# An attention block on one core: layer-norm tokens turned by VectorE, DMA and GpSimd in place of TensorE, and 231 blocks of exponentials on VectorE in place of 204

## The reference, cut to what matters

```python
h = _layernorm(x, axis=-1) * (1 + ca) + sa
q = jnp.einsum('bte,fe->btf', query, Wq)...          # query is h; k and v likewise
scores = jnp.einsum('bhtd,bhsd->bhts', q * scaling, k)
attn_w = jax.nn.softmax(scores, axis=-1)             # 4 x 32 x 2048 x 2048 exponentials
aw = aw[:, :, 0] - lam * aw[:, :, 1]
attn = jnp.einsum('bhts,bhsd->bhtd', aw, v)          # then an RMS norm per head pair, Wo
x = x + ga * attn_ref(h, ...)
h = _layernorm(x, axis=-1) * (1 + cb) + sb
x = x + gb * jnp.einsum('bsi,oi->bso', h, w_ternary * scale)
```

## Time and profile before

| what | us |
|---|---|
| median of 3 runs | 3610.86 (3609.04 to 3613.66) |
| the profiled execution, its own time | 3607.35 |
| its span in the profile | 3605.5 |
| ACT busy in it | 3534.4 (98%) |
| PE busy | 3405.9 (94%) |
| DVE busy | 2588.9 (72%) |
| POOL busy | 338.0 (9%) |

### The profile page before, as it was taken

How to read it: one execution, slowest core, us unless ns; L and a number is a source line. 1 busy time by engine, 2 the same in 40 slices (tenths; PEclk the granted TensorE clock), 3 DMA queues, 4 the chain that set the end, 5 groups by cost and what they waited for, 6 DMA issues and landing times. The chain is left out here.

```text
span 3605.5 us, 76890 instructions
## 1 busy us (share of the span) xinstructions
PE 3405.9 (94%) x32302; PEld 799.1 (22%) x32302; DVE 2588.9 (72%) x3808; ACT 3534.4 (98%) x2808; POOL 338.0 (9%) x229
## 2 busy tenths in 40 slices
PE   8999999999899999999999999999999999989998
PEld 5222112122122222222222222222221222211222
DVE  6687878863578687776367768677547888878886
ACT  5999999999999999999999999999999999999998
POOL 3010101010010100101001010100100000000001
PEclk9999999999999999999999999999999999999999
DMA  6111110111101111101111001111012110010000
GB/s 196 28 32 39 32 31 22 35 39 33 38 21 42 48 35 40 50 23 33 36 47 50 25 31 36 40 49 36 20 31 63 45 37 22 17 30 16 20 22 26
DMA packets 103700, 136.90 MB, mean 38 GB/s; under 512 B 9916, under 2 KB 88716, under 8 KB 103340
## 3 DMA queue, kind: packets, MB, share of 16 engines
q1 hardware_dynamic: 102524, 131.01, 12.9%
q10 hardware_dynamic: 816, 0.79, 0.1%
HBM read 72.50 MB, written 59.19 MB: 37 GB/s over the span
## 5 line engine op out<-in xcount | busy, mean ns | idle before, releaser
L1146 ACT ACTIVATE probs<-ps 128x1536 f32<-128x1536 f32 (+1 forms) x2732 | 3497.4, 1670 | 15.5 <-PE ps L1263 13.9
L1291 PE MATMUL ps<-probs,values 128*32 128x512 f32 x14600 | 2047.9, 606 | 4.9 <-DVE wmod_sb L1644 2.4
L1263 PE MATMUL ps<-queries,keys 25*128 25x512 f16 x7680 | 1003.9, 385 | 160.6 <-ACT probs L1146 142.0
L1263 PEld LDWEIGHTS ps<-queries,keys 25*128 25x128 f16 x7680 | 249.8, 91 | 1947.3 <-ACT probs L1146 1861.5
L1291 PEld LDWEIGHTS ps<-probs,values 128*32 128x32 f32 x14600 | 300.2, 108 | 416.9 <-issue 410.5
L1623 DVE TENSOR_SCALAR d_y<-ps 128x512 f32<-128x512 f32 x240 | 165.6, 690 | 295.4 <-PE ps L1263 284.7
L1708 DVE STREAM_TRANSPOSE seg_t<-ps 128x512 f32<-128x512 f32 x127 | 91.0, 716 | 356.9 <-PE ps L1291 356.4
L1060 POOL TENSOR_TENSOR seg_rs<-seg_ms,neg_half 128x16 f32<-128x16 f32 x64 | 185.7, 2901 | 1506.1 <-DVE seg_ms L1721 1506.1
L1640 DVE SCALAR_TENSOR_TENSOR wmod_sb<-wmod_sb 128x1024 f32<-128x1024 f32 x204 | 249.6, 1224 | 6.3
L1644 DVE SCALAR_TENSOR_TENSOR wmod_sb<-wmod_sb,gates 128x1024 f32<-128x1024 f32 x204 | 249.5, 1223 | 6.0
L1642 DVE SCALAR_TENSOR_TENSOR wmod_sb<-wmod_sb,d_y 128x1024 f32<-128x1024 f32 x204 | 249.3, 1222 | 5.3
(11 more groups left out here) (181 smaller groups left out, 1690.9 us busy)
## 6 DMA issues: line engine op xcount, KB each, us to landing
v_scr<-a_v SPq DMA_DIRECT2D x16, 1024.0 KB, 5.6
values<-v_scr SPq DMA_DIRECT2D x29, 512.0 KB
queries<-q_scr SPq DMA_DIRECT2D x116, 96.0 KB
keys<-k_scr SPq DMA_DIRECT2D x116, 96.0 KB
e_x<-in_x_dram SPq DMA_DIRECT2D x18, 512.0 KB, 5.2
attn_scr<-seg_o SPq DMA_DIRECT2D x254, 32.0 KB
e_attn<-attn_scr SPq DMA_DIRECT2D x31, 256.0 KB, 3.6
out_dram<-e_y SPq DMA_DIRECT2D x15, 512.0 KB, 3.3
```

What stands on the lines that cost most here:

```text
L1146: nc.scalar.activation(probs[:, s % PRING, at, :], ps[:, base + at.start:base + at.stop:at.step, :], ACT.Exp, scale=1.0 / SQUARE).then_inc ...
L1263: last = nc.tensor.matmul(ps[:, score_bank(n), :], keys[buf][at, u * P:(u + 1) * P], queries[buf][at, tc * CH:(tc + 1) * CH], start=True, ...
L1291: last = nc.tensor.matmul(pv[row:row + VW, :], values[buf][:, n % SEG_BANKS // HEADS, j // 2, :], probs_of(n), start=(i == 0), stop=(i == ...
```

## The change

- **Turning.** The two turning steps of every job in the main loop leave PE. DVE writes the normed tokens so that 128 features of four token blocks stand in a row (`by_square`), transposes all 32x32 squares in one instruction (`turn_normed`, 128x1024 into the new tile `turned`), SP issues 16 DMAs that put the squares into their places in `a_hT` or `e_hT` (`turn_squares`), and GpSimd applies scale and shift there (`scale_turned`, two instructions of 128x512). 27 jobs are turned so, one of them ahead of the loop.
- **Shares.** `shared(k)` gives two shares to every segment outside the last five of a turn body, the first and the last: 231 for 204. The first share comes from units 3 and 5. Each share has its own two tiles for the fraction and the whole part (`d_y`/`g_y`, `d_n`/`g_n`), part 1 is a plain subtraction, and part 3 of a share waits until the sums of the segment before are done (`pv_done`), since it is the first to write into the probabilities' tile.
- **Order.** The steps left in the two middle batches are spread over a body by single pieces; `segment_sums` is cut into three or four entries that may be put apart; statistics, normalisation and turning have due slots of their own. GpSimd has a list of its own (`pool_order_of`), in which nothing waits for `d_done`.

The two batch ends and the last segment are as before. The core of the diff:

```diff
-    D_UNITS = ((4, 6), (8, 10))
+    D_UNITS = ((3, 5), (8, 10))
...
-        light = {("a", 0): 1, ("a", 1): 1, ("a", 6): 2, ("a", 7): 2, ("e", 0): 2, ("e", 2): 1, ("e", 3): 1, ("e", 4): 2, ("e", 5): 2}
...
-        return 2 if sum(light.get(step, 3) for step in steps) <= 5 and not normed else 1
+        return 2
...
+            spread = [[NB + 14 * (PIECES * j + p) // 5 for p in range(PIECES)] for j in range(A_MADE + len(E_MADE))]
+            put("a", body + NC, [(), ()] + spread[0:4] + spread[6:8])
+            put("e", body - GP, spread[4:6] + [(), ()] + spread[8:10])
...
+            def turn_squares(kind, job):
...
+                sp.wait_ge(square_turned, TURN_OF[kind, job] + 1)
+                for row in range(P // 32):
+                    for col in range(P // 32):
+                        src = turned[32 * col:32 * col + 32, :, 32 * row:32 * row + 32]
+                        dst = hT[32 * row:32 * row + 32, :, :].rearrange("p c (n t) -> p (c n) t", n=BPC)[:, :, 32 * col:32 * col + 32]
+                        sp.dma_start(dst, src).then_inc(turn_done, DMA)
...
+            def scale_turned(kind, job, c):
...
+                    pool.wait_ge(turn_done, (TURN_OF[kind, job] + 1) * SQUARES * DMA)
+                nc.gpsimd.tensor_scalar(hT[:, c, :], hT[:, c, :], cols_sb[:, first + 1, c, m:m + 1], cols_sb[:, first, c, m:m + 1], ALU.mult, ALU.add).then_inc(done, 1)
...
-                        if shares:
-                            pool.wait_ge(d_done, shares)
...
+                V.transpose(turned[:, :, :].rearrange("p n f -> p (n f)"), normed[:, :, :].rearrange("p n e -> p (n e)")).then_inc(square_turned, 1)
...
-                    link.then(V.scalar_tensor_tensor(d_y[:, :], d_n, SHIFT, y, ALU.subtract, ALU.subtract))
+                    link.then(V.tensor_tensor(f, whole, f, ALU.subtract))
...
+                    if k:
+                        dve.wait_ge(pv_done, OPEN + k * NB)
```

More of the change, by code:

```diff
@@ L334, in put @@
             nonlocal clock
-            order.append(entry)
             clock += cost
[L337 to L342, removed]
+            order.append((clock, *entry))
+            if entry[0] == "sums":
+                later.extend((entry[2] + SUMS_AT, 0, SUMS_COST[part], ("rest", entry[1], part)) for part in range(1, sums_parts(entry[1])))
+            elif entry[0] == "rest" and entry[2] == 3:
+                later.append((slot_of((entry[1] + 1) * SEG_BANKS) + 12, clock + NORM_WAIT, 900, ("norms", entry[1])))
+            elif entry[0] in ("a_apply", "e_apply"):
+                later.append((slot_at(clock) + APPLY_AT, 0, 1600, ("turn", entry[0], entry[1])))
+            elif entry[0] == "read" and BLOCK_OF[entry[1]][2]:
+                share = BLOCK_OF[entry[1]][0]
+                due = min(GROUP_SLOT.get(GROUP_OF[n], ALL_SLOTS) for n in D_BLOCKS[share][2])
+                later.extend((due, 0, cost, ("share", share, part)) for part, cost in enumerate(SHARE_COST))
             elif entry[0] == "evacuate" and entry[1] == "a" and 2 <= entry[3] < 6:
@@ L414, in order_of, with pool_order_of, first_of, take @@
         if b < B - 1:
-            order.append(("sums", (b + 1) * GP * SEGS - 1))
-        return order
+            k = (b + 1) * GP * SEGS - 1
+            order.append((clock, "sums", k, 0))
+            order.extend((clock, "rest", k, part) for part in range(1, sums_parts(k)))
+        return order
+    TURN_WAIT = 12000
+    def pool_order_of(b):
+        order, scales, held, clock = [], [], [], 0
+        def first_of(until):
+            heads = [queue for queue in (scales, held) if queue and max(clock, queue[0][0]) < until]
+            return min(heads, key=lambda queue: max(clock, queue[0][0])) if heads else None
+        def take(queue):
+            nonlocal clock
+            ready, cost, task = queue.pop(0)
+            order.append(task)
+            clock = max(clock, ready) + cost
+        for at, what, *task in order_of(b):
+            while first_of(at):
+                take(first_of(at))
+            if what == "turn":
+                scales.extend((at + TURN_WAIT, 800, ("scale", task[0][0], task[1], c)) for c in range(EC))
+            elif what in ("a_stats", "e_stats") or what == "rest" and task[1] == 3:
+                order.append((what, *task))
+                clock = max(clock, at) + (2900 if what == "rest" else 1010)
+            elif what == "evacuate" and task[0] == "a" and 2 <= task[2] < 6:
+                held.append((at, 1900, ("split", task[1], task[2] - 2)))
+        while first_of(STARTS[-1] + 10 ** 9):
+            take(first_of(STARTS[-1] + 10 ** 9))
+        return order
+    TURNS = [("a", NC)]
+    for body in range(B * GP):
+        for _, kind, job, i, p in sorted((u, *step) for u, step in steps_of(body).items()):
+            if kind == "e" and i == 1 and p == PIECES - 1:
+                TURNS.append(("e", job))
+        if body + 1 < (B - 1) * GP:
+            TURNS.append(("a", body + 1 + NC))
+    TURN_OF = {turn: n for n, turn in enumerate(TURNS)}
     LAST_JOB = (B - 1) * NC
@@ L1044, in _ @@
             a_power(NC)
+            for c in range(EC):
+                scale_turned("a", NC, c)
             for b in range(B):
```

245 lines of the change are left out of this document (130 added, 115 removed).

## The result

| | before | changed |
|---|---|---|
| median | 3612.14 us (4 runs, 3609.04 to 3613.66) | 3667.74 us (4 runs, 3665.59 to 3669.44) |
| profiled execution, its span | 3607.35, 3605.5 us | 3665.59, 3663.9 us |
| granted TensorE clock, mean of the span | 0.998 | 0.986 |

The ratio is 1.0155, with an interval of 1.0137 to 1.0172: 55.6 us slower.

The account below looks back on a forecast made before the run. ACT was taken to set the pace, with PE following. 3607.35 - 23 (ACT) + 22 (DVE overflow) + 20 (POOL collisions) = 3626.4 us; the median lies 3.5 above: 3629.9, say 3629, range 3592 to 3650.

Parts of the forecast that it names:

- ACT, -23 us: On ACT, 54 exponentials go from three banks to two, saving 23 us, all of it on the path.
- the announced signs: ACT's span 50 to 60 us over 3467, PE's sums waiting tens of us for DVE, share parts up to 2 us.
- "Where that room is missing", +22 us: DVE segments with statistics, apply and turn overflow, so ACT waits: 26 jobs at 0.85 us, +22 us (0 to 68).
- The worked segment: First order excerpt's segment: DVE's stretch grows from 14.7 to 17.8 us, PE stands 3.1 us, ACT loses about 2.6.
- Rival A: The shares are free on DVE, which has 28% idle time: 3588 to 3603 us, chance 0.21.
- the objection to A: The last-batch bodies that carried 16 shares with hardly any ACT loss had neither splits nor turns.
- PE, 0: The turning products of 26 jobs leave PE's loop; they lie beside ACT, so the effect is 0.
- POOL beside the shares, +20 us: POOL's splits and scales collide with DVE's share parts: 41 us of DVE delay, half reaching ACT, +20 us (0 to 70).
- the lower end of a collision: Each collision of POOL with DVE was said to cost DVE 0.4 to 1.0 us; 0.4 is the lower end.
- DMAs, 0: 16 DMAs per job, 11.5 us with landing and scaling, are ready before PE needs the features: 0, bounds 0 to 3 us a job.
- D: Rival: PE waits for turned features if turn to scale takes over 17 us; 78 us more, 3700 us, chance 0.05.

Follow-up runs that it names:

- e3: The changed kernel with GpSimd's four splits held until the segment's shares on VectorE are done, scales left in place; 3655.16 us, ratio 1.0123.
- e4: The changed kernel with the planner's durations set from the profile (apply 1750 to 1400, turn 1600 to 1250 ns); 3640.08 us, ratio 1.0080.
- e2: The changed kernel with the 204 shares of before in their old segments, the turn and new order kept; 3654.38 us, ratio 1.0126.
- e1: The changed kernel with 8 matmuls by zeros ahead of TensorE's wait for VectorE's last share in 15 segments; 3643.15 us, ratio 1.0087.
- e8: e7 with 8 matmuls by zeros added ahead of the scores of the seventh slot of batches 1 to 3; 3603.13 us, ratio 0.9980.
- e7: The changed kernel with e3's held splits, e4's durations and a table of 213 shares; 3609.42 us, ratio 0.9997.
- e10: The changed kernel with all 231 shares, e4's durations, and the zero matmuls of e1 and e8; 3627.71 us, ratio 1.0040.

## Why the prediction was right in its sign and 39 us short

- *ACT, -23 us.* Right: 466 exponentials over two banks, work of 2266 x 1.343 + 466 x 0.917. But from the first to the last exponential it took 3565 us, 98 over the 3467 named, not 50 to 60. The page had the announced signs: 51.2 us of sums waiting for DVE's last share part, single parts up to 2.07 us, the turn at 1.24 us (forecast 1.26).
- *"Where that room is missing", +22 us.* The first step that failed, and not in its arithmetic on DVE. The worked segment came out as computed: from the read of unit 8 to the end of the second share

```profile
1113.90 0.69 DVE L1699 TENSOR_SCALAR g_y<-ps 128x512 f32<-128x512 f32 x1 [2.72 <-PE ps L1344]
...
1131.10 1.68 DVE L1721 SCALAR_TENSOR_TENSOR wmod_sb<-wmod_sb,g_n 128x1024 f32<-128x1024 f32 x1
```

  lie 18.9 us, where 17.8 were said and 0.9 are POOL's two collisions; PE stood 4.14 us where 3.1 were said. Two things failed behind it. The mean over the jobs: 26 x 0.85 took a third of one segment's loss, but PE waited 24 times for a last part, 2.1 us in the mean, and still 50.1 us in 24 waits with the splits held (e3). The price of a wait: in this segment ACT stood 4.83 us where 2.6 were said. The step also took an engine's spare time as usable: e4 shows that 28 us of the loss came from the order alone, with the same work. DVE stood at reads while share parts were ready, as the 2.72 us in the first line.
- *Batch 3.* Rival A read batch 3 of the earlier trace rows as evidence that 16 shares a body are free. That they were free before does not carry over: with the same number of shares batch 3 stalls 29.6 us in the changed kernel and 32.6 in e2, because the turn and the new order came into these bodies. The prediction named this as the objection to A, and it was right.
- *PE, 0.* The other step that failed, and wrong in kind: I priced PE's pauses by their length, and what follows a pause at nothing. The clock at the pauses costs again: e1 takes 24.6 us off with added matmuls. And the pieces that left PE were not idle ballast everywhere; at the start of batch 1 they had shortened a pause by the 1.66 us that they took, and matmuls in their place are worth 6 us over the three starts (e8 against e7).
- *POOL beside the shares, +20 us.* Mechanism right, and the size too as far as it was tried. The delay on DVE was put at 41 us and is 40.4; half of it was let through, and of the 24 us that e3 takes away 12.6 arrive. That the 16 us beside the scales pass on half as well was not tried. A scale takes 0.77 us at its shortest and 1.16 in the mean, for the 0.7 said, and the lower end of a collision was misread: 1.17 less twice 0.43 is 0.3 us, not 0.4. The Trainium skill ("SBUF — State Buffer", "Who interferes with whom") had the parts with two SBUF inputs take turns with POOL. That 1.68 us stand for 1.22 beside a scale agrees with it in kind; the 0.46 us added are less than a whole scale, so the row does not show that one waits out the other.
- *DMAs, 0.* Right in effect: the changed kernel's trace has no wait of PE for POOL's `a_hT` or `e_hT`. But the chain is longer than the 11.5 us said, close to the 17 from which D would have decided. In segment 2 of batch 3, where the turn starts at 2820.82, the timeline has

```profile
2822.14 10.54 SPq L825 DMA_DIRECT2D e_hT<-turned  x16
...
2834.20 2.17 POOL L1105 TENSOR_SCALAR e_hT<-e_hT,cols_sb 128x512 f32<-128x512 f32 x2 [10.90 <-DMA e_hT<-turned]
```

  so 10.5 us for 16 issues where 6.5 were said, and 15.5 us from the turn's start to the scales' end. The issues made it longer, 0.61 us each for 0.40; the landing, with the runs of 128 bytes that D held open, took 2.0 us where 3.6 were said.
- *The miss as a whole.* The sum had 42 us of added stalls, measured are 78; the remaining 3.6 us are the prologue's. PE's waits for the last share part rose by 46 us. That this is near the 42 is luck: held splits (e3) hardly change these waits, so they are mostly the overflow's, which was put at 22. ACT lost 32 us more than these waits; e1 puts the clock's part at some 25, and PE's waits for DVE's turn of the sums (`seg_t`) rose by 9. e10, with all 231 shares but without most of the falls and of the misplaced reads, lands at 3627.7 us, near the 3629 forecast. That does not confirm the two terms, since the forecast was for the changed kernel's own order.

## What to carry to other kernels

In this kernel, with TensorE busy 92% of the span, the pauses over 2.1 us were nearly all followed by work at half clock, and the shorter ones mostly not. So look at the granted clock in short stretches at the longest waits, and try cheap work in the pause. Work that an engine beside the critical one "has time for" should be checked against its order: give a planner durations from the trace, and see whether the engine waits with ready work queued behind it. Give a helper engine more work only in those segments whose last wait has room; here 20 of the 231 shares, VectorE's blocks of exponentials, made 61 of the 78 us of added stalls.

## What the runs showed of the hardware

- The granted clock of the changed kernel falls around the end of a pause of PE: at its 18 single pauses from 1.1 us before PE's next matmul to 1.8 us behind it. In the first example it is 1.00 (2.4 GHz) nearly to the end of the pause and 0.50 (1.2 GHz) for 3.4 us from there; elsewhere for 6.8. The pause's length alone does not tell: 2.24 us brought a fall in the changed kernel and none in e2, 2.20 none in e1; 1.61 and 2.09 us brought none in the changed kernel and one in e1. At 521.85 us of the changed kernel it fell at two pauses of 0.88 and 0.83 us:

```profile
519.00:521.00 2.00, 1.45 (x14) 0.35 (x14) 1.93 (x3) 2.00 (x3) 0.00 (x0) 1.00 0.13 19
521.00:523.00 2.00, 1.17 (x11) 0.23 (x8) 0.97 (x1) 2.00 (x2) 0.00 (x0) 0.71 0.32 51
523.00:525.00 2.00, 2.00 (x18) 0.19 (x14) 0.79 (x2) 0.89 (x2) 0.00 (x0) 0.50 0.31 47
```

- Matmuls that add zeros can keep it up: 2 us of them inside pauses of 2.2 to 4.1 us did so at 14 of 15 places in e1.
- POOL and DVE slow each other: a CAST takes 1.26 us in the mean of the changed kernel and 0.72 in e3, a share part with two SBUF inputs 1.68 for 1.22 beside a scale and at most 2.07.
- A DMA of 32 KB whose runs are 128 bytes took SyncE 0.61 us to issue (median of the 240 into `e_hT`, and of the 192 into `a_hT`) and 2.0 us to land.
